# More row sums taken off ScalarE's own accumulator, a shorter way for the first head, and a root in seven steps instead of nine

## The chip, the cores and the metric

The kernel runs as one program on one core of one Trainium2 chip. The time is the device time of that core in microseconds (us), lower is better. Times of the kernel before are the median of three runs; beside them stands one further run under the hardware profiler, and all rows below come from that one.

## The reference, cut to what matters

One transformer layer on x of shape 8 x 1024 x 256 (batches, tokens, features), 16 heads of width 16, all in float32:

```python
x = x + attention(layernorm(x))
x = x + ffn(layernorm(x))

def layernorm(x):  return (x - mean) / sqrt(var + 1e-5)

def attention(x):                       # per head: q, k, v of 1024 x 16
    q_rot, k_rot = rotate(q), rotate(k) # rotary tables cos, sin
    num = exp(q_rot @ k_rot.T / 4)
    den = sum(exp(q @ k.T / 4), axis=-1)      # of the plain q and k, over all keys
    attn = where(causal, num / den, 0)
    return (attn @ v, heads side by side) @ Wout + bout

def ffn(x):     # shared expert (256 -> 128 -> 256, squared relu), plus routed experts
    ...         # weighted by trunc(softmax of the top two logits), which is 0 below 1.0
```

So each head needs two tables of exponentials: the denominator's, full 1024 x 1024 and only summed by row, and the numerator's, of which the causal half is used.

## The kernel before

**Tiling.** A batch is cut into 4 units of 4 heads (`G`, `HG`); 8 batches make 32 units. A unit is 50 steps (`NSTEP`), each one tile of 128 x 1024 scores: 32 "den" steps (4 heads x 8 blocks of 128 query rows, all 1024 keys) and 18 "num" steps that hold the causal half of the numerators in five chunks (`CHUNKS`; chunks 0 to 3 have one step for each head, chunk 4 has two heads in a step). Per step TensorE (PE) writes the tile into one of three score tiles in PSUM (`RING` = 3), and ScalarE (ACT) takes the exponential. A tile may be written again when the exponential three steps earlier is done.

**Row sums of the denominators.** A den step has two forms. In the first (L571) ACT writes the exponentials back in place and gives the row sum by its accumulator, which adds an instruction that reads the accumulator out. In the second (L569), for steps named in `SUMMED`, ACT writes the exponentials into one of two tiles in SBUF (`sum_tiles`, `SUM_SLOTS` = 2), and VectorE (DVE) adds the halves and sums them with its own accumulator (L1055, `sum_den`). That instruction stands in DVE's program three steps later (`SUM_LAG`). ACT waits before it writes a sum tile until the sum before last has been taken. `SUMMED` lists, for each of six kinds of unit (units 0 to 3 of a batch, the very last unit, the very first one), which of the 32 dens are summed so: 278 in the whole kernel, 746 go by the accumulator.

**Other work around the steps.** All engines walk the same 50 steps in their own fixed program; nothing is decided at run time. `ORDER`, `ORDER_FIRST`, `ORDER_LAST` say how dens and numerator chunks alternate. `PV_STEPS` says at which step PE multiplies a piece of a numerator chunk with v; `TAKE_Y` when DVE takes that sum out of PSUM. `SIDE` says at which step a side tile (one PSUM bank, `side`) is made by PE and taken by DVE: v, q and k of the next unit ("qk" and "turn" for the plain and rotated forms), the output projection ("acc"), the second layernorm's transposes ("t2"), the router and the shared expert of the batch before. `STATS2`, `STATS1`, `BIAS`, `GAP`, `BRANCH`, `RECIPROCALS` place single jobs of DVE, GpSimd (POOL) and ACT. `BUSY` and `WARM_UP` put dummy matmuls on PE.

**q and k.** For 6 products per score the float32 q and k are split into three bfloat16 parts (high, middle, low) by DVE, the last subtraction by POOL (L477). The parts go to DRAM (`scratch`, L376 on SyncE's DMA queue, SP) and come back as rows of `stack` in the order that the contraction over 96 rows wants: 6 DMAs for q and 6 for k for each of the plain and rotated forms (L393), 24 in a unit.

**The start.** Before batch 0: DVE takes the statistics of x and the inverse root (`inverse_root`, L959 on), writes the normalized blocks `xn` (L994), PE transposes them (L696) with dummy matmuls between (L627), ACT copies them (L592); PE makes q and k (L706), DVE splits them (L1338 to L1342), SP sends the two halves (L418). When both have landed, SP and ACT each issue 6 fills for heads 0 and 1 (`first_fill`, L346), then SP 6 for heads 2 and 3 of q. DVE meanwhile turns q and k and splits them into the same tile `parts` (L1330 to L1352), the second halves wait in SP's queue behind the fills (L418), then come 6 fills of k for heads 2 and 3 and the 12 fills of the rotated stack (L393). DVE enters batch 0 when both rotated halves have been sent (`rot_sent`).

**The inverse root.** `inverse_root` adds EPS, makes a first guess by integer arithmetic (three instructions in all) and does three Newton steps of three instructions each, with a drain behind each.

## Time and profile before

| what | us |
|---|---|
| median of 3 runs | 1618.52 (1616.33 to 1618.64) |
| the profiled execution: its own time | 1615.4 |
| its span, first to last instruction | 1613.7 |
| ACT busy | 1559.3 |
| PE busy (modelled ends) | 1508.5 |
| DVE busy | 1022.8 |
| POOL busy | 470.4 |

The granted TensorE clock has a mean of 0.997 over the span. How to read the profile: a row of a timeline gives start, duration, engine, source line, what is written and read, a count of merged instructions and, in brackets, the idle time of the engine before it with what ended it. A duration of ACT begins when the instruction is taken in, so two neighbours overlap; what a step costs is the distance between starts, its pitch. "<-PE scores L648" names the releaser of a wait; "issue" is time in which the engine waited for nothing that the profile shows.

### The profile page before, as it was taken

What the parts mean: (1) busy time and instruction counts of PE and PEld (TensorE: products, weight loads), DVE (VectorE), ACT (ScalarE), POOL (GpSimd) and SP (SyncE); (2) the same over time, 40 slices, a digit from 0 to 9 for tenths busy, and PEclk for the clock granted to TensorE, in tenths of its full rate; (3) what the DMA queues carried; (4) which work ended last, traced back from release to release, by engine and by line L of the source; (5) the groups of instructions that cost most, each with busy time, mean ns of one, the idle gap of its engine ahead of it and who ended that gap; (6) DMA issues with size and microseconds to landing.
All of it is one profiled execution on the core that took longest, in us unless ns stands there. A gap on an engine that the chain in (4) does not pass through costs nothing.

```text
span 1613.7 us, 26958 instructions
## 1 busy us (share of the span) xinstructions
PE 1508.5 (93%) x8670; PEld 624.2 (39%) x8670; DVE 1022.8 (63%) x2567; ACT 1559.3 (97%) x2373; POOL 470.4 (29%) x857
## 2 busy tenths in 40 slices
PE   7989999999999999999999999999999999999988
PEld 6334433333333333333333333433333333333325
DVE  5454656766567675677656676676666766566626
ACT  2999999999999999999999999999999999999995
POOL 3332233222332323323233223322233222332210
PEclk9999999999999999999999999999999999999999
DMA  5522233421434314343234333343243431433310
GB/s 165 159 92 86 85 118 115 134 93 59 134 119 134 102 47 134 118 125 118 69 106 131 115 105 99 115 127 95 89 145 105 131 99 62 129 120 116 106 39 27
DMA packets 95397, 172.14 MB, mean 107 GB/s; under 512 B 15696, under 2 KB 82256, under 8 KB 83152
## 3 DMA queue, kind: packets, MB, share of 16 engines
q1 hardware_dynamic: 94656, 169.55, 33.2%
q8 instruction: 72, 1.18, 0.3%
q10 hardware_dynamic: 592, 0.79, 0.2%
q14 instruction: 77, 0.63, 0.1%
HBM read 111.55 MB, written 58.72 MB: 106 GB/s over the span
## 4 chain that ended last, share of the span: by engine, by line
ACT 73%; issue 11%; PE 9%; DVE 3%; SPq 2%; DMA 1%; POOL 1%; DVEq 1%; POOLq 0%; ACTq 0%
ACT scores L571 37%; ACT probs L581 23%; ACT sum_tiles L569 11%; PE scores L648 3%; PE y_ps L677 2%; ACT probs L583 2%; SPq L393 2%; DMA qk_parts<-parts 1%; PE side L687 1%; PE side L627 1%; PE scores L655 1%; DVEq L958 0%; POOL probs L470 0%; PE side L706 0%; DMA stack<-qk_parts 0%
## 5 line engine op out<-in xcount | busy, mean ns | idle before, releaser
L571 ACT ACTIVATE scores<-scores 128x1024 f32<-128x1024 f32 x746 | 810.7, 1167 | 18.5 <-PE scores L648 18.3
L648 PE MATMUL scores<-stack 96*128 96x512 bf16 x2048 | 576.7, 382 | 37.6 <-ACT probs L581 12.4
L581 ACT ACTIVATE probs<-scores 128x1024 f32<-128x1024 f32 x512 | 497.9, 1158 | 0.2
L477 POOL TENSOR_TENSOR parts<-rest,parts 128x512 bf16<-128x512 f32 x124 | 161.2, 1300 | 748.0 <-DVE parts L1025 719.5
L655 PE MATMUL scores<-stack 96*128 96x512 bf16 (+3 forms) x1536 | 330.5, 327 | 36.9 <-ACT scores L571 16.2
L470 POOL TENSOR_SCALAR_AFFINE_SELECT probs<-probs 128x256 f32<-128x256 f32 (+1 forms) x640 | 245.2, 411 | 344.5 <-ACT probs L583 181.9
L677 PE MATMUL y_ps<-probs,v_sb 128*32 128x512 f32 (+3 forms) x3072 | 328.1, 499 | 1.0
L648 PEld LDWEIGHTS scores<-stack 96*128 96x128 bf16 x2048 | 151.2, 97 | 445.7 <-ACT scores L571 136.7
L569 ACT ACTIVATE sum_tiles<-scores 128x1024 f32<-128x1024 f32 x278 | 315.0, 1209 | 0.2 <-PE scores L648 0.2
L1055 DVE SCALAR_TENSOR_TENSOR sum_tiles<-sum_tiles 128x512 f32<-128x512 f32 x278 | 208.9, 763 | 88.9 <-ACT sum_tiles L569 80.0
L571 ACT ACTIVATION_READ_ACCUMULATOR scores<-scores 128x1 f32 x746 | 252.4, 338 | 0.0
L655 PEld LDWEIGHTS scores<-stack 96*128 96x128 bf16 x1536 | 123.5, 97 | 252.7 <-ACT scores L571 68.3
L706 PE MATMUL side<-xnt,w_qk 128*128 128x512 f32 x248 | 128.1, 597 | 0.0
L1034 DVE COPY rest<-side 128x512 f32<-128x512 f32 x62 | 42.9, 691 | 124.5 <-PE side L706 109.4
L677 PEld LDWEIGHTS y_ps<-probs,v_sb 128*32 128x32 f32 x3072 | 60.7, 108 | 150.5 <-issue 127.8
L583 ACT ACTIVATE probs<-scores 128x1024 f32<-128x1024 f32 x64 | 68.5, 1232 | 0.3 <-PE scores L655 0.3
L687 PE MATMUL side<-w_v,xnt 128*128 128x256 f32 x256 | 66.0, 379 | 2.4 <-DVE rot L1035 2.4
L722 PE MATMUL side<-w_o,y_sb 128*128 128x256 f32 x240 | 64.2, 390 | 0.0
L1043 DVE TENSOR_TENSOR turned<-turned,sin_sb 128x512 f32<-128x512 f32 x62 | 50.6, 816 | 19.4 <-POOL parts L477 19.4
L1025 DVE CAST parts<-rest 128x512 bf16<-128x512 f32 x124 | 53.0, 427 | 9.4 <-issue 0.4
L1005 DVE COPY v_sb<-side 128x128 f32<-128x128 f32 x128 | 28.2, 283 | 43.0 <-PE side L687 42.9
L511 POOL TENSOR_TENSOR tokens<-tokens,bias 128x256 f32<-128x256 f32 x64 | 53.2, 845 | 0.0
(145 smaller groups left out, 1238.9 us busy)
## 6 DMA issues: line engine op xcount, KB each, us to landing
stack<-qk_parts SPq DMA_DIRECT2D x756, 128.0 KB, 2.6
qk_parts<-parts SPq DMA_DIRECT2D x127, 384.0 KB, 2.6
out<-x_mid SPq DMA_DIRECT2D x32, 256.0 KB, 2.9
tokens<-in_L_attn_x SPq DMA_DIRECT2D x7, 1024.0 KB, 5.5
stack<-qk_parts SPq DMA_DIRECT2D x18, 64.0 KB, 2.3
tokens<-in_L_attn_x SPq DMA_DIRECT2D x2, 512.0 KB, 4.5
probs<-in_L_attn_Wqkv SPq DMA_DIRECT2D x1, 512.0 KB, 5.8
cos_sb<-in_cos SPq DMA_DIRECT2D x1, 512.0 KB, 6.5
```

What stands on the lines that cost most here:

```text
L470: nc.gpsimd.affine_select(out=v, in_=v, compare_op=ALU.is_ge, fill=0.0, base=0, pattern=pattern, channel_multiplier=-1).then_inc(masked, 1)
L477: nc.gpsimd.tensor_tensor(parts[:, t % 2, 2, :], rest[:, :], parts[:, t % 2, 1, :], ALU.subtract).then_inc(low_ready, 1)
L569: nc.scalar.activation(sum_tiles[:, k % SUM_SLOTS, :], src, ACT.Exp, scale=SCALE).then_inc(exp_done, 1)
L571: nc.scalar.activation(src, src, ACT.Exp, scale=SCALE, accum_out=den[:, g % 2, i, j:j + 1]).then_inc(exp_done, 1)
L581: nc.scalar.activation(probs[:, chunk % 2, j, :], src, ACT.Exp, scale=SCALE).then_inc(exp_done, 1)
L583: nc.scalar.activation(probs[:, chunk % 2, j:j + 2, 0:HALF], src.rearrange("p (a n) -> p a n", a=2), ACT.Exp, scale=SCALE).then_inc(exp_do ...
L648: mm = nc.tensor.matmul(tile[:, half * HALF:(half + 1) * HALF], q[:, j, i * P:(i + 1) * P], k[:, j, half * HALF:(half + 1) * HALF], start= ...
L655: mm = nc.tensor.matmul(tile[:, col:col + n], k[:, h, i * P:(i + 1) * P], q[:, h, q0:q0 + n], start=True, stop=True)
L677: mm = nc.tensor.matmul(y_ps[32 * j:32 * j + 32, o0:o0 + n], v_sb[:, i, h, :, :], probs[:, (5 * g + c) % 2, j, col:col + n], start=piece i ...
L687: mm = nc.tensor.matmul(side[:, i * D:(i + 1) * D], xnt[:, k, (2 * t + i) * P:(2 * t + i + 1) * P], w_v[:, k, :], start=k == 0, stop=k == ...
L706: mm = nc.tensor.matmul(side, w_qk[:, k, g, :], xnt[:, k, half * HALF:(half + 1) * HALF], start=k == 0, stop=k == KC - 1)
L1055: nc.vector.scalar_tensor_tensor(tile[:, 0:HALF], tile[:, 0:HALF], 0.0, tile[:, HALF:C], ALU.add, ALU.add, accum_out=den[:, g % 2, i, j:j ...
```

## The change

1. **Tables.** `SUMMED` names 344 dens instead of 278. With it `ORDER`, `ORDER_FIRST`, `ORDER_LAST`, `PV_STEPS`, `TAKE_Y`, `SIDE`, `RECIPROCALS`, `STATS1`, `STATS2`, `BIAS`, `GAP`, `BRANCH`, `BUSY` and `WARM_UP` get other numbers. By unit 0, 1, 2, 3, last, first the counts of summed dens go from 8, 6, 8, 14, 5, 7 to 7, 11, 9, 17, 8, 8.
2. **Start.** The six parts of head 0 of q and of k go from `parts` straight to the stack (`head_fill`), when the split is done, without DRAM. Heads 1 to 3 come from DRAM by 12 DMAs on SP (`heads_fill`). The rotated parts get a place of their own (`rot_parts`, in the second probability buffer), so the split of the rotated form waits for no DMA, and DVE enters batch 0 when the first head's rows are there.
3. **Root.** One Newton step with a scaled guess, then one step of third order: 3 + 4 instructions for 9.

```diff
+ROOT_SCALE = 0.375 ** 0.2
-ORDER = [5, (0,), 6, (1,), 2, (2,), 6, (3,), 6, (4,), 7]
-ORDER_FIRST = [15, (0,), 2, (1,), 3, (2,), 0, (3,), 1, (4,), 11]
+ORDER = [5, (0,), 4, (1,), 4, (2,), 6, (3,), 6, (4,), 7]
+ORDER_FIRST = [15, (0,), 0, (1,), 1, (2,), 1, (3,), 5, (4,), 10]
 SUMMED = [
-    (7, 11, 12, 16, 17, 20),
+    (2, 3, 5, 9, 11, 13, 19, 21, 24, 25, 26),
 SIDE = [
-    {0: ("xt", 1), 2: ("acc", 3), 4: ("xt", 2), 5: ("xt", 3), 9: ("qk", 0), 15: ("ffn", 4), 17: ("ffn", 5),
-     19: ("turn", 1), 22: ("qk", 2), 31: ("turn", 3), 34: ("ffn", 6), 39: ("ffn", 7)},
+    {0: ("xt", 1), 2: ("xt", 2), 4: ("acc", 3), 6: ("xt", 3), 8: ("qk", 0), 12: ("ffn", 4), 15: ("turn", 1),
+     19: ("ffn", 5), 22: ("qk", 2), 28: ("ffn", 6), 33: ("turn", 3), 35: ("ffn", 7)},
-WARM_UP = (22, 3, 3, 30, 22)
-BUSY = {(1, 4): 1, (1, 5): 1, (1, 6): 1, (1, 7): 1, (2, 7): 1, (2, 8): 1}
+WARM_UP = (19, 0, 3, 30, 13)
+BUSY = {(1, 3): 1, (1, 4): 1, (1, 5): 1, (1, 6): 1, (1, 7): 1, (1, 8): 1, (2, 6): 1, (2, 7): 1, (2, 8): 1}
-STATS2 = (1, 25)
+STATS2 = (1, 33)
...
+        rot_parts = probs[:, 1, 0:2, :].rearrange("p a n -> p (a n)").bitcast(BF16)[:, 0:2 * PARTS * HALF]
...
-        def first_fill(engine, a, term, heads, stacked):
+        def head_fill(engine, a, term):
             part = (Q_TERMS, K_TERMS)[a][term]
+            rows = parts[a * DH * HG:(a + 1) * DH * HG:HG, :, part, :]
+            engine.dma_start(stack[term:ROWS:TERMS, 0, 0, a, 0:C].rearrange("d (f t) -> d f t", f=2), rows).then_inc(first_stacked, 16)
+        def heads_fill(engine, a, term):
+            part = (Q_TERMS, K_TERMS)[a][term]
             src = scratch[0].rearrange("c s (d h) t -> c s d (h t)", h=HG)
-            cols = slice(heads * HG // 2 * C, (heads + 1) * HG // 2 * C)
-            engine.dma_start(stack[term:ROWS:TERMS, 0, 0, a, cols], src[part, a][:, cols]).then_inc(stacked, 16)
+            engine.dma_start(stack[term:ROWS:TERMS, 0, 0, a, C:HG * C], src[part, a][:, C:HG * C]).then_inc(plain_stacked[0], 16)
...
@@ SP @@
+            for term in range(TERMS):
+                head_fill(sp, 0, term)
             for half in range(2):
                 sp.wait_ge(first_sent[half], 16)
             sp.sem_inc(plain_sent, 32)
-            for term in range(TERMS):
-                first_fill(sp, 0, term, 0, first_stacked)
-            for term in range(TERMS):
-                first_fill(sp, 0, term, 1, plain_stacked[0])
+            for a in range(2):
+                for term in range(TERMS):
+                    heads_fill(sp, a, term)
             sp.wait_ge(low_ready, 4)
             first_parts(1, 1, rot_sent)
-            for term in range(TERMS):
-                first_fill(sp, 1, term, 1, plain_stacked[0])
             fill_stacks(0, 0, 1, rot_sent, rot_stacked)
@@ ACT @@
+                if j == 0 and first and chunk == 1:
+                    act.wait_ge(rot_sent, 32)
...
-            for half in range(2):
-                act.wait_ge(first_sent[half], 16)
+            act.wait_ge(low_ready, 2)
             for term in range(TERMS):
-                first_fill(act, 1, term, 0, first_stacked)
+                head_fill(act, 1, term)
@@ PE @@
-                            if step == ("den", HG // 2, 0):
+                            if step == ("den", 1, 0):
                                 pe.wait_ge(plain_stacked[0], FILLS * 16)
...
-            pe.wait_ge(first_sent[1], 16)
+            pe.wait_ge(low_ready, 2)
@@ DVE, inverse_root @@
-                for i in range(3):
-                    nc.vector.scalar_tensor_tensor(a, y, -0.5, y, ALU.mult, ALU.mult)
-                    settle()
-                    nc.vector.tensor_tensor(a, a, v, ALU.mult)
-                    settle()
-                    nc.vector.scalar_tensor_tensor(result if i == 2 else y, a, 1.5, y, ALU.add, ALU.mult)
-                    settle()
+                nc.vector.scalar_tensor_tensor(a, y, -0.5 * ROOT_SCALE, y, ALU.mult, ALU.mult)
+                nc.vector.tensor_tensor(a, a, v, ALU.mult)
+                nc.vector.scalar_tensor_tensor(y, a, 1.5 * ROOT_SCALE, y, ALU.add, ALU.mult)
+                nc.vector.tensor_tensor(a, y, y, ALU.mult)
+                nc.vector.tensor_tensor(a, a, v, ALU.mult)
+                nc.vector.scalar_tensor_tensor(v, a, -10 / 3 * ROOT_SCALE ** 2, a, ALU.add, ALU.mult)
+                nc.vector.scalar_tensor_tensor(result, v, 5 * ROOT_SCALE ** 4, y, ALU.add, ALU.mult)
...
@@ DVE, before batch 0 @@
-                dve.wait_ge(first_sent[half], 16)
-                first_split(half, rot_of[half])
-            dve.wait_ge(rot_sent, 32)
+                first_split(half, rot_of[half])
+            for half in range(2):
+                dve.wait_ge(first_sent[half], 16)
+            dve.wait_ge(first_stacked, FILLS * 16)
```

(In the new root each instruction still has its drain behind it.)

**Where instructions stand, three places.** SP's queue from the first sent halves on, before; the shapes are the destination's rows and columns, `qk_parts` is `scratch`:

```order
L418 DMA qk_parts<-parts 128x3x512 x2
L346 DMA stack<-qk_parts 16x2048 x12
L418 DMA qk_parts<-parts 128x3x512
L346 DMA stack<-qk_parts 16x2048 x6
L393 DMA stack<-qk_parts 16x4096 x12
L376 DMA qk_parts<-parts 128x3x512 x3
```

And now:

```order
L426 DMA qk_parts<-parts 128x3x512 x2
L348 DMA stack<-parts 16x2x512 x6
L354 DMA stack<-qk_parts 16x3072 x12
L426 DMA qk_parts<-probs 128x3x512
L401 DMA stack<-qk_parts 16x4096 x12
L384 DMA qk_parts<-parts 128x3x512 x3
```

The queue has as many DMAs as before; six read `parts` directly, and the second rotated half now stands behind 18 fills and not behind 12, with none between it and the rotated stack.

PE from its first dummy matmul to the first scores, before:

```order
L627 MATMUL side<-ident 128x128 x22
L696 MATMUL scores<-ident,xn 128x128 x4
L627 MATMUL side<-ident 128x128 x3
L706 MATMUL scores<-xnt,w_qk 128x512 x4
L627 MATMUL side<-ident 128x128 x52
L648 MATMUL scores<-stack 128x512 x4
L706 MATMUL side<-xnt,w_qk 128x512
```

(the rows of 4 transposes and 3 dummies come four times) and now:

```order
L635 MATMUL side<-ident 128x128 x19
L704 MATMUL scores<-ident,xn 128x128 x16
L635 MATMUL side<-ident 128x128 x3
L714 MATMUL scores<-xnt,w_qk 128x512 x4
L635 MATMUL side<-ident 128x128 x43
L656 MATMUL scores<-stack 128x512 x2
L714 MATMUL side<-xnt,w_qk 128x512
```

There are 21 dummy matmuls fewer, none between the transposes, and the first side tile stands one step earlier.

ACT in the second half of unit 1 (here of batch 0), from the third numerator chunk (before: from the fourth den behind it) on, before:

```order
L569 ACTIVATE sum_tiles<-scores 128x1024 x2
L571 ACTIVATE scores,den<-scores 128x1024
L581 ACTIVATE probs<-scores 128x1024 x4
L571 ACTIVATE scores,den<-scores 128x1024
L569 ACTIVATE sum_tiles<-scores 128x1024
L571 ACTIVATE scores,den<-scores 128x1024 x4
L583 ACTIVATE probs<-scores 128x2x512 x2
L571 ACTIVATE scores,den<-scores 128x1024 x12
```

And now:

```order
L590 ACTIVATE probs<-scores 128x1024 x4
L576 ACTIVATE sum_tiles<-scores 128x1024
L578 ACTIVATE scores,den<-scores 128x1024 x5
L590 ACTIVATE probs<-scores 128x1024 x4
L576 ACTIVATE sum_tiles<-scores 128x1024
L578 ACTIVATE scores,den<-scores 128x1024
L576 ACTIVATE sum_tiles<-scores 128x1024
L578 ACTIVATE scores,den<-scores 128x1024 x2
L576 ACTIVATE sum_tiles<-scores 128x1024
L592 ACTIVATE probs<-scores 128x2x512 x2
L576 ACTIVATE sum_tiles<-scores 128x1024 x2
L578 ACTIVATE scores,den<-scores 128x1024 x10
```

Dens that went through L571 (now L578) go through L569 (now L576), six in this stretch where three stood; never more than two follow one another.

## Rows read from the trace of the kernel before

**Rows 1.** ACT's groups: line, operation, tiles, count | busy us, mean ns | idle before.

```profile
L571 ACT ACTIVATE scores<-scores 128x1024 f32<-128x1024 f32 x746 | 810.7, 1167 | 18.5 <-PE scores L648 18.3
...
L569 ACT ACTIVATE sum_tiles<-scores 128x1024 f32<-128x1024 f32 x278 | 315.0, 1209 | 0.2 <-PE scores L648 0.2
```

**Rows 2.** Timeline of ACT in unit 3 of batch 5.

```profile
1158.74 1.25 ACT L571 ACTIVATE scores<-scores 128x1024 f32<-128x1024 f32 x1
...
1159.77 3.99 ACT L581 ACTIVATE probs<-scores 128x1024 f32<-128x1024 f32 x4
1163.38 1.29 ACT L569 ACTIVATE sum_tiles<-scores 128x1024 f32<-128x1024 f32 x1
1164.28 1.30 ACT L571 ACTIVATE scores<-scores 128x1024 f32<-128x1024 f32 x1
```

**Rows 3.** Timeline of ACT: the first and the last of the 1600 steps.

```profile
34.56 1.01 ACT L571 ACTIVATE scores<-scores 128x1024 f32<-128x1024 f32 x1 [10.84 <-PE scores L648]
...
1590.46 1.03 ACT L571 ACTIVATE scores<-scores 128x1024 f32<-128x1024 f32 x1
```

**Rows 4.** Timeline of all engines at the start.

```profile
5.26 8.07 PE L627 MATMUL side<-ident 128*128 128x128 f32 x44 [5.26 <-POOL ident L454]
...
11.54 1.38 DVE L994 TENSOR_SCALAR xn<-tokens,mean_var,rstd 128x256 f32<-128x256 f32 x4
...
13.17 0.60 PE L696 MATMUL scores<-ident,xn 128*128 128x128 f32 x4
...
17.87 3.67 PE L706 MATMUL scores<-xnt,w_qk 128*128 128x512 f32 x8
...
24.11 0.69 DVE L1342 TENSOR_TENSOR parts<-y_sb,parts 128x512 bf16<-128x512 f32 x1 [0.51 <-issue]
...
27.45 7.75 SPq L346 DMA_DIRECT2D stack<-qk_parts  x12
27.46 4.04 ACTq L346 DMA_DIRECT2D stack<-qk_parts  x6
...
34.66 1.16 POOL L539 TENSOR_TENSOR parts<-y_sb,parts 128x512 bf16<-128x512 f32 x1 [3.16 <-DVE parts L1334]
...
38.59 0.69 DVE L1034 COPY rest<-side 128x512 f32<-128x512 f32 x1 [4.02 <-DMA qk_parts<-parts]
...
40.04 8.26 SPq L393 DMA_DIRECT2D stack<-qk_parts  x12
...
41.54 1.01 ACT L571 ACTIVATE scores<-scores 128x1024 f32<-128x1024 f32 x1 [2.90 <-PE scores L648]
```

**Rows 5.** Timeline of ACT: the first numerator steps of the kernel.

```profile
52.74 3.76 ACT L581 ACTIVATE probs<-scores 128x1024 f32<-128x1024 f32 x4
```

**Rows 6.** Busy time (count) of PE, PEld, DVE, ACT, POOL by stretch; PEclk, DMA share, GB/s.

```profile
1057.99:1106.44 48.45, 45.61 (x274) 17.90 (x273) 34.24 (x98) 48.45 (x78) 13.31 (x25) 1.00 0.41 126
...
93.30:96.70 3.40, 3.40 (x6) 1.32 (x6) 3.10 (x5) 2.79 (x4) 1.20 (x2) 0.50 0.36 120
```

**Rows 7.** The page: DVE's group that takes the sums.

```profile
L1055 DVE SCALAR_TENSOR_TENSOR sum_tiles<-sum_tiles 128x512 f32<-128x512 f32 x278 | 208.9, 763 | 88.9 <-ACT sum_tiles L569 80.0
```

**Rows 8.** Timeline of DVE in unit 1 of batch 5: the second layernorm's last root instruction.

```profile
1086.14 0.17 DVE L974 SCALAR_TENSOR_TENSOR rstd<-root 128x8 f32<-128x8 f32 x1
1086.39 1.38 DVE L994 TENSOR_SCALAR xn<-x_mid,mean_var,rstd 128x256 f32<-128x256 f32 x4
```

**Rows 9.** Timeline of SP around the change from batch 5 to batch 6.

```profile
1193.38 0.50 SPq L376 DMA_DIRECT2D qk_parts<-parts  x1
1196.64 8.28 SPq L393 DMA_DIRECT2D stack<-qk_parts  x12
```

**Rows 10.** Timeline of POOL there: the low part of the rotated second half.

```profile
1186.76 1.16 POOL L477 TENSOR_TENSOR parts<-rest,parts 128x512 bf16<-128x512 f32 x1 [4.09 <-ACT probs L581]
```

**Rows 11.** Timeline of ACT there: third step of batch 6, and its first numerators.

```profile
1205.24 1.01 ACT L571 ACTIVATE scores<-scores 128x1024 f32<-128x1024 f32 x1 [0.18 <-PE scores L648]
...
1208.18 2.85 ACT L581 ACTIVATE probs<-scores 128x1024 f32<-128x1024 f32 x3
```

More of the change, by code:

```diff
@@ L418, in first_parts @@
                 sp.dma_start(scratch[kind, :, :, :, half * HALF:(half + 1) * HALF].rearrange("c s r t -> (s r) c t"),
-                             parts[:, half, :, :]).then_inc(sent, 16)
+                             (parts, rot_parts)[kind][:, half, :, :]).then_inc(sent, 16)
             sp.sem_inc(out_sent, 1)
@@ L538, in _ @@
                 pool.wait_ge(middle_ready, half + 3)
[L539 removed]
+                nc.gpsimd.tensor_tensor(rot_parts[:, half, 2, :], rest_of[half], rot_parts[:, half, 1, :], ALU.subtract
                                         ).then_inc(low_ready, 1)
```

62 lines of the change are left out of this document (32 added, 30 removed), and 17 rows, old and new, of tables (PV_STEPS, SUMMED).

## The prediction

> **What bounds the kernel now.** First I read the busy shares in the table: ACT is busy 1559.3 of 1613.7 us, more than any other engine. ACT's groups [rows 1] then show that it hardly waits: its main group idled 18.5 us in all, of which 10.84 stand before the very first score tile [rows 3]. So I took the timeline of ACT and looked at the distance between starts, since durations overlap. In an undisturbed stretch [rows 2] a den through the accumulator (L571) takes 1159.77 - 1158.74 = 1.03 us until the next step starts, four numerator steps 3.61, so 0.90 each, and a den through a sum tile (L569) 1164.28 - 1163.38 = 0.90. 746 steps of the first kind and 1600 - 746 = 854 of the others [rows 1] make 746 x 1.03 + 854 x 0.90 = 1537 us. From the first step to the start of the last are 1555.9 us [rows 3], some 1538 less the last step's own, so about 19 us in the 1600 steps are losses. Known among them are 2.90 at 41.54 [rows 4] and, in the stretch of 3.4 us in which the granted clock was 0.50, the lower of TensorE's two levels, 3.40 - 2.79 = 0.6 or more of idle ACT [rows 6]. The kernel's time is therefore three parts: 34.6 us until the first exponential, 1556 of steps paced by ACT, and 23 behind them, a chain through DVE, PE and ACT.
>
> **Sums moved.** 344 - 278 = 66 dens change from L571 to L569. Each saves ACT 1.03 - 0.90 = 0.13 us (0.126 with one more digit of the same starts: 1.029 and 0.903), so 66 x 0.126 = **8.3 us**, all on the path, since ACT sets it. The cost lies on DVE: 208.9 / 278 = 0.75 us for each [rows 7], 50 us over the kernel. The fullest unit is unit 1: DVE was busy 34.24 of 48.45 us [rows 6] and gets 5 sums more, so 38.0 us or 78%. That is cover enough on average; ACT pays only if a sum tile is wanted again before DVE has come to it. ACT's order shows never more than two such dens in a row, with numerators or accumulator dens behind them, as before.
>
> As a counterweight, the Trainium skill ("ScalarE: Activation LUTs", What ACT_TABLE_LOAD costs) gives an activation with immediate scale and bias 186 ns + 0.833 ns a column and 93 ns of overlap between neighbours. For 1024 columns that is 946 ns a step; with the trace's 1.03 for the accumulator form the saving would be an estimate of 0.083 a den, 5.5 us for 66. The trace does not agree: its pitch is 0.90, for numerators and sum tiles alike, and I go by the trace.
>
> **The start.** Five steps, each from [rows 4] unless said. (a) The root loses two instructions. One takes 1086.39 - 1086.14 = 0.25 us from start to start [rows 8], so `xn` starts 0.5 us earlier, at 11.05, and its first pair is done at 11.05 + 0.69 = 11.7. (b) PE's first dummies ended at 13.33 and held the transposes back. With 19 for 22 they end 3 x 2 records earlier, at the warm rate some 0.14 us each, so about 12.5: 0.8 us. Without the dummies between them the four blocks of transposes, 4.70 us up to the q and k product at 17.87, become a chain of 0.6 us of PE and 0.7 us of DVE for the third and fourth block, with some 0.3 us of hand-over each; I work it out as 3.6 us. Both together bring the product forward by 1.9 us; the bounds are 0.8 (only the dummies at the front count) and 2.5 (the path through DVE alone). (c) The parts of q and k are ready at 24.80 before, so at 22.9. Until now the fills then waited for two landings and started at 27.45. Now SP sends the second half and then issues 6 head fills, ACT its 6, from 23.3 and 23.0 on. A fill's issue takes 7.75 / 12 = 0.65 us, so the last ends near 27.2. Before, the last issue on ACT ended at 31.50 and the first exponential came 3.06 later; now that gives **30.3** instead of 34.56. The new fills move 1 KB pieces instead of 4 KB, from SBUF and not from DRAM; no row shows such a fill, so between 1 us less and 2 us more for the landing. (d) Behind them 12 fills of the other heads are issued until 27.2 + 7.8 = 35.0 and land by 37.4; step 8, which needs them, comes at 30.3 + 8 x 1.03 = 38.5, and PE wants them a little earlier: no loss, or up to 1 us. The wait of 2.90 at 41.54 goes: DVE entered batch 0 at 38.59, held by the rotated parts, while PE waited for it to take the first side tile. Its chain and POOL's last low part (35.82) come 1.9 earlier, so DVE starts at 34.0; PE meets the next side tile at step 5, near 35, so some tenths remain. (e) What is late next is the rotated stack. The second rotated half is now behind 18 fills: issued at 35.0 (its low part is ready at 33.9), landed and waited for 2.7 us as before, then 12 fills in 8.3 us from 37.7 to 46.0, landed near **48.1**; before they were issued from 40.04 to 48.30. ACT would be ready for the first numerator at 30.3 + 13 x 1.03 + 2 x 0.90 + 0.4 = 45.9 and waits for it until about 48.8. Before, it came at 52.74 [rows 5]. The start as a whole thus gives **4.0 us**, not the 4.3 plus 2.9 that (c) and (d) would; its bounds are 2.0 (if (b) gives 0.8, and landings are slower) and 5.0.
>
> **Losses in the steps.** Three things can add or take. ACT's 0.18 us before the third step of a batch [rows 11] with the longer pitches around it recur at each batch, and they are PE's: side tiles stand there in both kernels. One more dummy matmul stands in unit 2 beside steps where PE is just ahead, and three places in unit 1 likewise; one is about 0.14 x 2 = 0.28 us. In the first unit numerator chunks now follow each other sooner, and chunk 2 at step 24 needs v's product of chunk 0, of which the last piece stands on PE at that same step. I take 0.5 us for the first unit and 0.1 to 0.15 for each of seven batches, together **+1.3 us**. The lower bound is -5 (most of the small waits vanish), the upper +7 (1 us a batch).
> The step for the rotated half of the next batch's first unit moves from 31 to 33, 1.9 us later. That costs nothing: POOL's low part was done at 1187.92 [rows 10], but SP sent it at 1193.38, behind the plain fills, [rows 9], so 5.4 us of room. Its fills ended at 1204.92 and the numerator ran at 1208.18 [rows 11]; landing takes 2 to 3 us, so there is about a microsecond in hand, and this does not change, as the plain half (step 22) stays where it was.
>
> **The end.** Behind the last exponential one root stands on the chain: **-0.5 us**. In the other batches the root is on DVE beside ACT and worth nothing. The last unit's new order ends on 11 dens instead of 7, with the same five end tiles in the loop; I see no gain or loss above 0.5 in it.
>
> **The sum.** -8.3 - 4.0 + 1.3 - 0.5 = **-11.5 us**. On the profiled execution: span 1613.7 to 1602.2, its own time 1615.4 to 1603.9. That execution is 3.1 us below the median of the three runs, 1618.52, for which I forecast **1607.0**.
>
> **Rivals.**
> (1) *The start gives back more.* If fills out of SBUF in 1 KB pieces are slow, or the rotated stack comes only as before (48.30 issued), the start is worth 0.5 to 1: 1610. For it speaks that the queue of SP is as long as before; against it that its waits for landings before the fills are gone.
> (2) *PE takes part of the saving.* PE is busy 45.61 of 48.45 us in unit 1 [rows 6], and with ACT 0.63 us faster there only 2.2 us are left. If half of the 8.3 is waited for at PE, 1611. Against it: ACT did not idle in that stretch at all (48.45 of 48.45), and PE's ends are modelled.
> (3) *Slower: DVE too late for the sum tiles.* In unit 1 the layernorm block (5 us of DVE) moves from step 25 to 33, in front of the sums of steps 35 and 37, and a third follows at 40. If PE's transposes hold DVE up between them, the sum of step 35 is not taken when ACT wants its tile. The price is the delay itself, once in each of seven batches. It cancels the whole gain from 12.8 / 7 = 1.8 us on; at 3 us it gives 1618.5 - 12.8 + 21 = 1627. Against it: DVE's program has nothing that waits between step 28 and this block, so DVE can run it early and be through before step 35.
> (4) *The clock.* Fewer dummies run at the start, and PE idles for up to 1 us or more before the first scores. The trace shows the clock at 0.50 for 3.4 us at 93.3, amid work, at a price of 0.6 us or more on ACT [rows 6]. One such stretch more at 1 us gives 1608; at the start, where PE is on the path, the q and k product of 3.67 us [rows 4] at half the clock takes that much more, and gives 1611. The Trainium skill ("TensorE: Matmul & The Clock Gate", Part 1: The HAM clock gate) says that the clock halves when the array has been idle and comes back with work; the row at 93.3, with PE busy 3.40 of 3.40 us, does not look like idleness, so I give it little.
>
> **How the numbers follow.** Forecast 0.62 (own range 1603 to 1610), rival 1 0.12, rival 2 0.13, rival 3 0.05, rival 4 0.08. The range 1601.5 to 1612.5 takes in the forecast's bounds, rivals 1, 2 and 4, and the scatter of 2.3 us between the three runs; outside are rival 3 and the extremes. About 0.2% (3.2 us) is what a measurement can tell from no change, so faster means below 1615.3: 0.91. Within 0.2% 0.05, where several bounds meet; slower 0.04, which is rival 3.
>
> **What the profile after would show.** ACT's in-place group at 680 and the sum group at 344; pitches of 1.03 and 0.90 unchanged; the first exponential near 30.3; the first numerator near 48.8 with a wait of some 3 us on the stack in front of it; idle of ACT in the later batches no more than before; `xn` 0.5 us earlier; DVE busy some 50 us more, less 34 root instructions of 0.17. It is wrong if ACT waits for DVE's sums in unit 1, if the first numerator comes after 51, or if pitches of the new sums are longer than 0.90.

## The result, and the profile after

| | before | after |
|---|---|---|
| median | 1617.42 us (4 runs, 1614.39 to 1618.64) | 1601.70 us (4 runs, 1600.98 to 1603.35) |
| the profiled execution: its own time | 1615.4 | 1600.98 |
| its span | 1613.7 | 1599.4 |
| first exponential / first numerator | 34.56 / 52.74 | 29.21 / 47.45 |
| last step's start to the end of the span | 23.29 | 22.70 |
| ACT / DVE / POOL / PE busy | 1559.3 / 1022.8 / 470.4 / 1508.5 | 1551.9 / 1064.9 / 506.7 / 1508.3 |

The ratio is 0.9908, with an interval of 0.9896 to 0.9919. The medians are 15.7 us apart (the ratio makes it 14.9), where 11.5 were forecast. The time lies just inside the range, 0.2 us above its lower end. The two profiled executions are 14.4 us apart; the other 1.3 us are what the medians lie above them, 2.0 before and 0.7 after.

The groups of the page after, ACT's two kinds of dens and DVE's sums (line, engine, operation, tiles, count | busy, mean ns | idle before), to be held against [rows 1, 7]:

```profile
L578 ACT ACTIVATE scores<-scores 128x1024 f32<-128x1024 f32 x680 | 752.9, 1225 | 10.4 <-PE scores L656 10.2
...
L576 ACT ACTIVATE sum_tiles<-scores 128x1024 f32<-128x1024 f32 x344 | 405.0, 1243 | 0.0
...
L1070 DVE SCALAR_TENSOR_TENSOR sum_tiles<-sum_tiles 128x512 f32<-128x512 f32 x344 | 257.3, 756 | 87.6 <-ACT sum_tiles L576 81.2
```

66 dens changed sides, DVE took 48.4 us more of sums, and ACT never once idled before a sum tile. Of the 10.4 us of idle before L578, 7.9 stand before the first step. A den through the accumulator still takes 1.029 us from its start to the next, every other step 0.903.

The start, timeline of all engines (to be held against [rows 4, 5]):

```profile
11.06 2.92 DVE L1009 TENSOR_SCALAR xn<-tokens,mean_var,rstd 128x256 f32<-128x256 f32 x8
...
15.47 3.67 PE L714 MATMUL scores<-xnt,w_qk 128*128 128x512 f32 x8
...
22.02 4.07 ACTq L348 DMA_DIRECT2D stack<-parts  x6
...
26.52 7.71 SPq L354 DMA_DIRECT2D stack<-qk_parts  x12
...
28.58 0.60 PE L656 MATMUL scores<-stack 96*128 96x512 bf16 x2
...
37.23 7.44 SPq L401 DMA_DIRECT2D stack<-qk_parts  x12
...
46.81 0.61 PE L663 MATMUL scores<-stack 96*128 96x512 bf16 x2 [3.59 <-DMA stack<-qk_parts]
...
47.45 1.02 ACT L590 ACTIVATE probs<-scores 128x1024 f32<-128x1024 f32 x1 [1.93 <-PE scores L663]
...
49.96 1.02 ACT L590 ACTIVATE probs<-scores 128x1024 f32<-128x1024 f32 x1 [1.49 <-PE scores L663]
```

Everything comes earlier, by 2.4 us at the product for q and k and by 5.3 at the first exponential and at the first numerator. The last two rows show something that the prediction had not expected at this place: after the wait for the stack, one numerator step is 2.5 us from the next instead of 0.90. The stretch behind it (busy time and count of PE, PEld, DVE, ACT, POOL; granted clock, DMA share, GB/s) shows why:

```profile
47.35:50.76 3.41, 3.41 (x7) 1.25 (x6) 0.00 (x0) 1.82 (x2) 0.00 (x0) 0.50 0.36 120
```

PE had idled 3.59 us for the rotated stack, and then runs at the lower level of its clock, busy all the time, with ACT busy only 1.82 of 3.41 us.

I took all 1600 steps apart: the start of each to the start of the next, less the undisturbed pitch of its kind in the kernel before (1.029 and 0.903, for all runs alike). What is left is called losses below.

| us | before | after | difference |
|---|---|---|---|
| first exponential at | 34.56 | 29.21 | -5.35 |
| 66 pitches of 0.126 less | | | -8.3 |
| losses, batch 0, unit 0 | 3.81 | 6.50 | +2.69 |
| losses, batch 0, unit 1 | 2.15 | 0.94 | -1.21 |
| losses, all other units | 12.17 | 10.56 | -1.61 |
| behind the last step's start | 23.29 | 22.70 | -0.59 |

They add up to the 14.4 within rounding. All losses together are 18.1 before and 18.0 after. Of the 6.5 us in unit 0 after, 3.4 stand behind the first numerator; before, it was 0.6 of 3.8.

### The profile page after: what moved, and what is told of

The parts are those of the page before. It is cut to its first block, busy times and chain, and to the rows that moved or that the text cites. A ratio compares the mean times of both kernels' runs of the same rounds, so it can differ in the third digit from the quotient of the medians.

```text
span 1599.4 us, 27029 instructions
## 1 busy us (share of the span) xinstructions
PE 1508.3 (94%) x8670; PEld 626.1 (39%) x8670; DVE 1064.9 (67%) x2665; ACT 1551.9 (97%) x2307; POOL 506.7 (32%) x857
## 4 chain that ended last, share of the span: by engine, by line
ACT 72%; issue 14%; PE 11%; DVE 1%; SPq 1%; DVEq 0%; DMA 0%; POOL 0%; ACTq 0%; POOLq 0%
ACT scores L578 33%; ACT probs L590 22%; ACT sum_tiles L576 15%; PE scores L656 3%; ACT probs L592 2%; PE scores L663 2%; PE side L695 2%; PE y_ps L685 2%; PE side L635 1%; SPq L354 0%; SPq L401 0%; PE side L714 0%; DVEq L966 0%; SPq L348 0%; PE scores L843 0%
## 5 line engine op out<-in xcount | busy, mean ns | idle before, releaser
L578 ACT ACTIVATE scores<-scores 128x1024 f32<-128x1024 f32 x680 | 752.9, 1225 | 10.4 <-PE scores L656 10.2
L590 ACT ACTIVATE probs<-scores 128x1024 f32<-128x1024 f32 x512 | 504.4, 1212 | 4.8 <-PE scores L663 4.2
L576 ACT ACTIVATE sum_tiles<-scores 128x1024 f32<-128x1024 f32 x344 | 405.0, 1243 | 0.0
L484 POOL TENSOR_TENSOR parts<-rest,parts 128x512 bf16<-128x512 f32 x124 | 175.5, 1415 | 689.2 <-DVE parts L1040 689.2
L477 POOL TENSOR_SCALAR_AFFINE_SELECT probs<-probs 128x256 f32<-128x256 f32 (+1 forms) x640 | 270.4, 450 | 352.5 <-ACT probs L592 179.0
L1070 DVE SCALAR_TENSOR_TENSOR sum_tiles<-sum_tiles 128x512 f32<-128x512 f32 x344 | 257.3, 756 | 87.6 <-ACT sum_tiles L576 81.2
L578 ACT ACTIVATION_READ_ACCUMULATOR scores<-scores 128x1 f32 x680 | 269.7, 397 | 0.0
L592 ACT ACTIVATE probs<-scores 128x1024 f32<-128x1024 f32 x64 | 69.1, 1242 | 0.1
L1058 DVE TENSOR_TENSOR turned<-turned,sin_sb 128x512 f32<-128x512 f32 x62 | 44.0, 710 | 19.9 <-POOL parts L484 18.8
L714 PEld LDWEIGHTS side<-xnt,w_qk 128*128 128x128 f32 x248 | 46.6, 191 | 14.3 <-DVE v_sb L1020 0.3
```

The costliest lines, as they stand in the source:

```text
L477: nc.gpsimd.affine_select(out=v, in_=v, compare_op=ALU.is_ge, fill=0.0, base=0, pattern=pattern, channel_multiplier=-1).then_inc(masked, 1)
L484: nc.gpsimd.tensor_tensor(parts[:, t % 2, 2, :], rest[:, :], parts[:, t % 2, 1, :], ALU.subtract).then_inc(low_ready, 1)
L576: nc.scalar.activation(sum_tiles[:, k % SUM_SLOTS, :], src, ACT.Exp, scale=SCALE).then_inc(exp_done, 1)
L578: nc.scalar.activation(src, src, ACT.Exp, scale=SCALE, accum_out=den[:, g % 2, i, j:j + 1]).then_inc(exp_done, 1)
L590: nc.scalar.activation(probs[:, chunk % 2, j, :], src, ACT.Exp, scale=SCALE).then_inc(exp_done, 1)
L592: nc.scalar.activation(probs[:, chunk % 2, j:j + 2, 0:HALF], src.rearrange("p (a n) -> p a n", a=2), ACT.Exp, scale=SCALE).then_inc(exp_do ...
```

## The experiments

They ran in three groups of four, e1 to e4, e5 to e8 and e9 to e12, each group on one chip with its own runs of the kernel before; the ratios are against those. Spans, waits and losses are those of the one profiled execution of each.

**e1: the new places with the old list of sums.** The changed kernel with the lines of `SUMMED` put back (278 sums):

```diff
-    (2, 3, 5, 9, 11, 13, 19, 21, 24, 25, 26),
+    (7, 11, 12, 16, 17, 20),
```

and the other five lines likewise.

> The changed kernel with the old list of summed dens (278 again), everything else new. If each summed den is worth the difference of ACT's pitches (1.029 - 0.903 = 0.126 us), the 66 dens go back to the accumulator and the span grows by 8.3 us, from 1599.4 to about 1607.7; the first exponential stays at 29.2 and losses of ACT stay near 18. If the rest of the tables (order, side tiles) carry the gain and the sums little, the span stays within 3 us of 1599.4.

Measured: 1641.36 us, ratio 1.0137 (1.0117 to 1.0158): 40 us slower than the changed kernel, not 8. Losses are 49.8 us; in batches 1 to 7 unit 1 loses 4.6 to 4.8 us each where the changed kernel loses 0.02. The timeline in unit 1 of batch 6:

```profile
1297.47 0.69 DVE L1070 SCALAR_TENSOR_TENSOR sum_tiles<-sum_tiles 128x512 f32<-128x512 f32 x1 [1.52 <-ACT sum_tiles L576]
...
1298.99 4.04 ACT L590 ACTIVATE probs<-scores 128x1024 f32<-128x1024 f32 x4
...
1299.17 0.64 DVE L1001 BATCH_NORM_AGGREGATE mean_var<-stats 128x2 f32<-128x6 f32 x8
...
1304.00 1.09 PE L738 MATMUL side<-ident,xn 128*128 128x128 f32 x4 [3.05 <-DVE xn L1009]
...
1305.98 1.01 ACT L578 ACTIVATE scores<-scores 128x1024 f32<-128x1024 f32 x1 [2.95 <-PE scores L656]
```

And the same place in the changed kernel:

```profile
1266.93 0.64 DVE L1001 BATCH_NORM_AGGREGATE mean_var<-stats 128x2 f32<-128x6 f32 x8
...
1269.97 4.05 ACT L590 ACTIVATE probs<-scores 128x1024 f32<-128x1024 f32 x4
...
1270.42 1.38 DVE L1009 TENSOR_SCALAR xn<-x_mid,mean_var,rstd 128x256 f32<-128x256 f32 x4
...
1271.79 0.60 PE L738 MATMUL side<-ident,xn 128*128 128x128 f32 x4
```

Against the same four numerators of ACT, DVE begins the layernorm block 3.04 us before them in the changed kernel, and 0.18 us behind them in e1. The first row of e1 shows what holds it, a sum that waits 1.52 us for ACT: the old list sums the dens 16 and 17, here steps 28 and 29, and these two sums stand in DVE's program directly ahead of the block. Not the number of sums decides, but whether one that must wait for ACT stands ahead of work that PE waits for.

**e2: the new list of sums with the old places.** The kernel before with nothing but the new `SUMMED` (344 sums).

> The kernel before with the new list of 344 summed dens and nothing else. Pitch theory: span 1613.7 - 8.3 = 1605.4, losses of ACT still 18. Rival: the new sums need the new order and the moved side tiles, and without them DVE comes too late for its two sum tiles; then ACT shows waits with DVE as the releaser, 1 us or more a batch, and the span is 1610 to 1625.

Measured: 1653.71 us, ratio 1.02 (1.0169 to 1.0231), losses 67.1. The sums alone save 8.3 us of ACT's pitches and make this kernel some 37 us slower (1653.71 against 1617.08; one of its four executions took only 1645.88). ACT's group, and the place in unit 3 where it idles (batch 5):

```profile
L569 ACT ACTIVATE sum_tiles<-scores 128x1024 f32<-128x1024 f32 x344 | 367.0, 1109 | 12.2 <-DVE sum_tiles L1055 11.8 <-PE scores L648 0.3
```

```profile
1193.39 0.69 DVE L1034 COPY rest<-side 128x512 f32<-128x512 f32 x1 [2.65 <-PE side L706]
...
1197.05 0.68 DVE L1055 SCALAR_TENSOR_TENSOR sum_tiles<-sum_tiles 128x512 f32<-128x512 f32 x1
...
1197.83 1.02 ACT L569 ACTIVATE sum_tiles<-scores 128x1024 f32<-128x1024 f32 x1 [1.68 <-DVE sum_tiles L1055]
```

Here the wait of rival 3 can be seen: a side tile that comes late from PE (2.65) holds DVE, the sum is queued behind its split, and ACT waits 1.68 us for its sum tile, in seven of eight batches. In unit 1 more is lost, 3.8 to 5.3 us in six of the batches; there PE waits some 2.2 us for DVE's `x_mid`. The list of sums is all that was changed, so the sums bring this about; which of them holds `x_mid` back was not traced. In batch 6:

```profile
1304.85 1.13 PE L722 MATMUL side<-w_o,y_sb 128*128 128x256 f32 x4 [2.21 <-DVE x_mid L1116]
```

This run also shows something about the start, which is here the same code as in the kernel before:

```profile
33.02 1.01 ACT L571 ACTIVATE scores<-scores 128x1024 f32<-128x1024 f32 x1 [10.12 <-PE scores L648]
```

The first exponential comes 1.54 us earlier than the 34.56 of before. The granted clock rose at 8.9 and not at 11.4, the product for q and k started at 17.05 and not at 17.87, and the last fill on ACT's queue landed 1.6 us behind the end of its issue and not 2.4. So the profiled execution of before had a late start, and a part of what the start seems to gain against it is scatter.

**e3: the start alone.** The kernel before with part 2 of the change (`head_fill`, `heads_fill`, `rot_parts`, the new waits) and the new `WARM_UP`; root and tables old.

> The kernel before with the new start alone (head 0 straight from SBUF, rotated parts apart, fewer dummy matmuls), old tables and old root. The first exponential should come at about 29.7 (29.2 plus the 0.5 us of the root, as the dummies no longer hold the transposes back). If the first numerators then are bound by the rotated stack, SP's queue decides: it lands near 47.2 and the first numerator comes near 48, against 52.74 before: 4.5 to 5 us gained. If the gain of the start came through the new order of the first unit, this one gains at most 2.

Measured: 1613.24 us, ratio 0.9968 (0.9955 to 0.9981): 5.2 us faster by the ratio, 3.8 by the medians, 3.2 by the spans. The first exponential comes at 30.05, the first numerator at 49.95, against 29.21 and 47.45 with everything. The difference between the two kernels grows from 0.8 to 2.5 us mainly through one place:

```profile
35.46 1.53 PE L695 MATMUL side<-w_v,xnt 128*128 128x256 f32 x4 [2.79 <-DVE rot L1043]
...
37.88 1.01 ACT L578 ACTIVATE scores<-scores 128x1024 f32<-128x1024 f32 x1 [3.75 <-PE scores L656]
...
40.04 1.01 ACT L578 ACTIVATE scores<-scores 128x1024 f32<-128x1024 f32 x1 [1.04 <-PE scores L656]
```

The old table has v's side tile at step 3 and PE waits there for DVE, still at the rotated split; the new one has it at step 5. Behind the idle of PE the granted clock is 0.50 from 36.05 to 39.46.

**e4: the root alone**, in the kernel before.

> The kernel before with the shorter root alone. Adding up instructions (2 fewer of 0.24 us, once at the start and once at the end) gives 1.0 us. The other reading is that the 22 dummy matmuls, which ended at 13.3 while the first blocks were ready at 12.3, swallow the first half: then the first exponential stays at 34.56 and only the tail shortens, from 23.3 to 22.8, 0.5 us in all.

Measured: 1615.41 us, ratio 0.9985 (0.9976 to 0.9995); the profiled pair differs by 1.5 us. At the end the half microsecond is there: 22.80 behind the last step's start instead of 23.29. At the start `xn` comes 0.46 earlier:

```profile
11.08 1.43 DVE L1002 TENSOR_SCALAR xn<-tokens,mean_var,rstd 128x256 f32<-128x256 f32 x4
12.68 0.60 PE L697 MATMUL scores<-ident,xn 128*128 128x128 f32 x4
```

but PE's 22 dummies still stand ahead of the transposes and hold them until 12.68, instead of 13.17. That they end earlier at all is not the root's doing: the granted clock rose at 10.3 in this execution and at 11.4 in that of before. The first exponential came at 33.39, 1.17 earlier than in before, where I had expected no change; e2, with the old root, came to it at 33.02, so this is the scatter of the start and not the root. With the old dummies the root stays hidden at the start.

**e5: 66 sums fewer, places kept.** The changed kernel with 66 dens taken out of the new lists and none put elsewhere, for instance

```diff
-    (2, 3, 5, 9, 11, 13, 19, 21, 24, 25, 26),
+    (2, 5, 11, 19, 24, 26),
```

> The changed kernel with 66 of its 344 summed dens simply dropped from its own lists (5 of 11 in unit 1, 3 of 17 in unit 3, 3 in the last and 2 in the first unit), so 278 again, and no sum at a place where none stood. Theory: a sum is worth 0.126 us on ACT and nothing else; the span grows by 8.3 us to 1607.7 and ACT's losses stay within 1 us of 18.0. Rival: taking sums away moves DVE's work as well and brings losses back, as the old list did; then losses grow by several us and the span passes 1612.

Measured: 1611.82 us, ratio 0.9961 (0.9947 to 0.9976). Its span is 1608.8, 9.4 more than the changed kernel's: 8.3 of pitches, 0.8 of losses, 0.3 at the end. The pitches are the same, 1.0295 and 0.9034, so a sum on DVE is worth 0.126 us where its place is free. The prediction had two prices for the 66 sums, 8.3 us by the trace's pitches and an estimate of 5.5 by the Trainium skill ("ScalarE: Activation LUTs", What ACT_TABLE_LOAD costs); the run agrees with the trace.

**e6: two sums moved.** The changed kernel, 344 sums, two of unit 1 in other places (steps 28 and 29 of the unit instead of two behind the block):

```diff
-    (2, 3, 5, 9, 11, 13, 19, 21, 24, 25, 26),
+    (2, 3, 5, 9, 11, 13, 16, 17, 24, 25, 26),
```

> The changed kernel, with two of unit 1's eleven summed dens in another place: dens 16 and 17 (steps 28 and 29) instead of 19 and 21 (steps 35 and 37). The count is the same, 344. Theory: DVE takes the sum of step 29 at its place 32, right in front of the second layernorm (place 33), and must wait there for ACT to reach step 30, so the layernorm comes some 3 us later, PE waits for its first block at step 34 and ACT runs dry: unit 1 loses 4 to 5 us in each of 7 batches, part of it through a halved clock, and the span is 1599.4 + 30 = 1630 or so. Rival: the loss with the old list came from the sums as a whole (their number in units 0 and 3, or the pace of ACT), then two moved sums cost under 5 us in all.

Measured: 1632.84 us, ratio 1.0079 (1.005 to 1.0107): 31 us more than the changed kernel for two numbers of a list (16 sums, two in each batch), with 3.6 to 5.4 us lost in unit 1 of each of the batches 1 to 7 and the granted clock at 0.50 for 3.4 or 6.8 us there. In batch 5:

```profile
1096.32 0.69 DVE L1070 SCALAR_TENSOR_TENSOR sum_tiles<-sum_tiles 128x512 f32<-128x512 f32 x1 [1.41 <-ACT sum_tiles L576]
...
1098.02 0.64 DVE L1001 BATCH_NORM_AGGREGATE mean_var<-stats 128x2 f32<-128x6 f32 x8
...
1102.51 1.08 PE L738 MATMUL side<-ident,xn 128*128 128x128 f32 x4 [2.71 <-DVE xn L1009]
...
1104.49 1.01 ACT L578 ACTIVATE scores<-scores 128x1024 f32<-128x1024 f32 x1 [2.61 <-PE scores L656]
```

The same rows as in e1, with every other table as in the changed kernel. The two sums alone bring e1's loss in unit 1 back, and that is its cause.

**e7: PE kept busy in its gap.** The changed kernel with 16 dummy matmuls ahead of PE's wait for the rotated stack:

```diff
+                            if first and g == 0:
+                                keep_busy(16, y_ps)
```

> The changed kernel with 16 dummy matmuls on PE (into the bank of the head products, not yet in use) in front of its wait for the first rotated stack, where PE idled 3.6 us and the granted clock then fell to 0.50 for 3.4 us. Theory: the idle time brings the fall; with PE busy the clock stays at 1.00, the two waits of 1.5 and 0.75 us behind the first numerator go, and the losses of the first unit fall from 6.5 to about 4 us, the span by 2.5 to 1597. Rival: the fall has nothing to do with the idle time (before the change it came at 93.3, amid work) and stays, or comes a little later, at the same price: span 1599 to 1600.

Measured: 1603.17 us, ratio 0.99 (0.988 to 0.9919). The granted clock is 1.00 from 8.7 us on and through all 1600 steps, and the waits behind the first numerator are 0.27 and 0.27 instead of 1.49 and 0.75:

```profile
48.16 1.02 ACT L590 ACTIVATE probs<-scores 128x1024 f32<-128x1024 f32 x1 [2.64 <-PE scores L663]
49.45 1.02 ACT L590 ACTIVATE probs<-scores 128x1024 f32<-128x1024 f32 x1 [0.27 <-PE scores L663]
```

```profile
47.35:50.76 3.41, 3.25 (x11) 1.45 (x12) 0.35 (x1) 2.07 (x3) 0.00 (x0) 1.00 0.52 180
```

So at this place the fall follows PE's idle time. Unit 0 of batch 0 lost 5.6 us instead of 6.5, forecast 4. The time itself did not come down: in this execution the 12 fills were issued in 8.29 us and not in 7.44, which brought the first numerator 0.7 later, and ACT's longer pitches (last section) come to some 2.3 us.

**e8: two fills on ACT's queue.** The changed kernel, in which ACT issues the last two of the 12 fills of heads 1 to 3:

```diff
-                for term in range(TERMS):
+                for term in range(TERMS - 2 * a):
...
+            for half in range(2):
+                act.wait_ge(first_sent[half], 16)
+            for term in range(TERMS - 2, TERMS):
+                heads_fill(act, 1, term)
```

> The changed kernel with the last two of the twelve fills for heads 1 to 3 issued by ACT, which has nothing to issue between 26.1 and 28.7, instead of SP. Theory: the first numerator is bound by SP's queue of single issues of 0.63 us; two fewer let the second rotated half go out when its low part is ready (33.0 instead of 34.3), the rotated stack lands near 45.5 and the first numerator is exponentiated at 46.2 instead of 47.45: 1.2 us less. Rival: the bound is the transfers themselves; then landings only bunch and the first numerator stays at 47.4.

Measured: 1602.94 us, ratio 0.9897 (0.9877 to 0.9917). SP sends the rotated half at 33.44 instead of 34.27, and the first numerator comes at 46.47, a wait of 0.54 instead of 1.93:

```profile
46.47 1.02 ACT L590 ACTIVATE probs<-scores 128x1024 f32<-128x1024 f32 x1 [0.54 <-PE scores L667]
```

PE idled 2.21 us before it and the clock did not fall there. It fell at 86.1, for 6.8 us, behind idle times of PE of at most 0.42:

```profile
84.40:91.20 6.80, 5.96 (x13) 1.61 (x14) 5.25 (x11) 6.55 (x9) 1.56 (x2) 0.63 0.17 58
91.20:98.00 6.80, 6.80 (x33) 2.98 (x32) 4.43 (x10) 5.33 (x9) 1.88 (x2) 0.87 0.17 59
```

Unit 0 lost 3.5 instead of 6.5 us, unit 1 then 2.9 instead of 0.9, so two thirds of the 3 us were given back.

**e9: the three put together.** e8's edit, nine dummies at e7's place, and the dummies of `BUSY` in unit 1 of batch 0 too:

```diff
-                if not first and (unit_of(b, g), s) in BUSY:
+                if (not first or g == 1) and (unit_of(b, g), s) in BUSY:
```

> The changed kernel, in which ACT issues the last two of the twelve fills for heads 1 to 3 (so the rotated half and the rotated stack behind it leave SP's queue some 0.9 us earlier), PE gets nine dummy matmuls ahead of its wait for the rotated stack, and the dummies that units 1 and 2 have in every other batch also stand in unit 1 of batch 0. Theory, the clock falls because PE idled: first numerator near 46.5 instead of 47.45, granted clock 1.00 behind it and through unit 1 of batch 0; the losses of unit 0 of batch 0 come down from 6.5 to about 3 us and those of unit 1 stay near 0.9, so 3 us less than the unchanged control of this call. Rival, a fall somewhere in batch 0 comes anyway and only moves: less than 1 us.

Measured: 1599.90 us (1599.45 to 1601.59), ratio 0.9883 (0.9868 to 0.9898), 2.7 below the control e12 of the same group, whose five runs all lie above all five of these; 3 were expected. The clock is 1.00 through all 1600 steps, in the two stretches in which it fell in the kernels above as well:

```profile
47.35:50.76 3.41, 3.23 (x13) 1.19 (x11) 1.29 (x3) 2.87 (x4) 0.00 (x0) 1.00 0.34 115
```

```profile
84.40:91.20 6.80, 6.61 (x28) 3.03 (x28) 5.28 (x11) 6.80 (x9) 1.53 (x1) 1.00 0.17 58
91.20:98.00 6.80, 6.57 (x40) 2.27 (x37) 5.02 (x12) 6.80 (x12) 1.93 (x2) 1.00 0.19 61
```

Which of the three edits keeps the clock up in the second stretch is not shown: e7, without the dummies of unit 1, had 1.00 there too, and so had the changed kernel.

The first numerator came at 47.13, not at 46.5. The fills began at 36.20, 1.0 earlier than in the changed kernel, but the last of them landed 2.8 us behind its issue instead of 2.1. Losses of unit 0 are 4.5, of unit 1 0.9.

**e10: 14 sums more.** The changed kernel with dens 9 and 13 of unit 0 summed too, in batches 1 to 7:

```diff
-    (6, 7, 11, 15, 24, 25, 28),
+    (6, 7, 9, 11, 13, 15, 24, 25, 28),
```

> The changed kernel with two more dens of unit 0 summed by DVE (dens 9 and 13 in order, steps 17 and 25 of the unit) in batches 1 to 7: 14 sums more, 358 in all. Theory, a sum is worth 0.126 us wherever no instruction of DVE that waits for PE or ACT is caught behind it and ahead of a step that PE needs: 14 x 0.126 = 1.8 us less than the control, losses of unit 0 unchanged at about 0.6 us a batch. Rival, unit 0 has no room left either, and DVE's side tile at step 19 or 28 comes late: losses in unit 0 grow by 0.3 us a batch or more, which takes the gain back.

Measured: 1602.75 us, ratio 0.99 (0.9885 to 0.9915), the same as the control's 1602.61. In the profiled pair, which ran at the same pitches, its span is 1.1 us less: 1.8 of pitches, 0.4 by an earlier start, less 0.8 more of losses (0.71 instead of 0.59 in a typical unit 0: step 26 takes 0.1 to 0.2 longer) and 0.3 at the end. So the trace has part of the 1.8, and the losses grow by 0.12 a batch, less than half of what the rival asked for; in the medians of five runs nothing of it shows. Whether 14 more sums are worth a microsecond stays open.

**e11: e9 and e10 together.**

> Both edits together: the shorter start with its dummies, and 14 sums more. Theory: the two act in different places and add up, about 4.5 us less than the control, near 1597. Rival: 2 us or less, if either edit gives nothing.

Measured: 1600.63 us (1598.41 to 1602.38), ratio 0.9884 (0.9868 to 0.99). The profiled execution, 1596.6 us of span, is the shortest of all; its first numerator stands at 45.99, the losses of unit 0 of batch 0 at 3.5:

```profile
45.99 1.02 ACT L590 ACTIVATE probs<-scores 128x1024 f32<-128x1024 f32 x1 [0.47 <-PE scores L667]
```

The median is 2.0 below the control, where 4.5 were expected, and not below e9's. The start's gain is there in both, that of the 14 sums in neither median.

**e12: the changed kernel once more**, the control of that group.

> The changed kernel unchanged, as the control of this call. Expected: 1600 to 1603, ratio to the kernel before near 0.990, first exponential 29.2, first numerator 47.5, granted clock 0.50 behind it. If ACT's distance between starts differs here from the 1.0295 us of the first execution, that is the scatter between executions, 1.5 to 2.5 us over 1600 steps.

Measured: 1602.61 us (1602.39 to 1603.13), ratio 0.9898 (0.9883 to 0.9912). The first exponential comes at 29.59, the first numerator at 47.70, and behind it the clock is at 0.50 again, now from 48.5 on:

```profile
48.60:51.90 3.30, 3.30 (x7) 1.27 (x6) 0.83 (x2) 1.23 (x3) 0.00 (x0) 0.50 0.21 68
```

## Why the prediction was right, and where it was off

The time is in the stated range, but by 0.2 us, and it lies below the forecast's own 1603 to 1610; no rival covers it, since all four make the kernel slower than forecast. The mechanisms below were right in the main. But the start, the losses and the step from the profile to the median all came out better than their terms, and the four executions spread over 2.4 us, two of them below 1601.5. That the median fell on the inner side of the bound is luck.

**What bounds the kernel**: right. ACT's pitches carried the sum, and with them the main term.

**Sums moved, -8.3**: right. The pitches are unchanged, 66 of them changed kind, and e5 gives the same 8.3 the other way round. DVE's price was 48.4 us, forecast 50.

**The start, -4.0**: its mechanism right, its size short by 1.3 and 0.3 beyond its own bound of 5.0; the first numerator came at 47.45 and not at 48.8. Against e4, whose start is the old one with the new root, the gain at the first numerator is 4.4 (51.84 to 47.45), so up to 0.9 of the 5.3 is the late start of the one execution of before. (a) `xn` at 11.06, as worked out. (b) was worth 2.4, not 1.9. The chain from the first transpose to the product takes 15.47 - 11.90 = 3.57, as worked out, but the dummies were over at 11.9 and not at 12.5, because the granted clock rose at 9.8 in this execution and at 11.4 in that of before. In e12 it rose at 11.0, and the first exponential came 0.37 later than in after. (c) The landing of a fill out of SBUF, the unknown of that step, took some 2.0 us from its issue, and 2.3 in the old form from DRAM: not slower, which closes rival 1. The rows of the first head were there at 27.6, and the first scores came at 28.58: PE's own dummies, which run until then, took the last microsecond. Fewer of them there was not tried. (d) The wait of 2.90 is gone, and four waits of 0.15 to 0.18 are left. e3 shows that this part belongs to the new tables and not to the new start: with the old ones a wait of 3.75 stands there. I had put it down to the earlier split alone. (e) was right in what is late next, the rotated stack: landed at 46.76, forecast 48.1, since (b) and (c) came earlier and the fills took 7.44 instead of 8.3. The wait in front of it was 1.93 us, forecast 3.

**Losses, +1.3**: this is the term that was mis-sized, it came out at -0.1. For the later batches the forecast of 0.1 to 0.15 each fits: a typical batch has 1.33 before and 1.43 after. For batch 0 it was wrong in both directions. Unit 0 lost 2.7 more instead of 0.5; 1.7 of it is the stretch of half clock behind PE's idle time (e7), which the prediction had looked for before the first scores and not before the first numerator. Elsewhere 3.3 came back: 1.2 in unit 1 of batch 0, where the stretch at 93.3 that I had read [rows 6] was not there after, 1.4 in unit 2 of batch 2, where before had a like one at 533.6, and 0.8 in the last unit. I had left their price in the sum without asking whether they would stay, and had read it too low: ACT waited 0.61 us in the stretch at 93.3 and 0.53 more right behind it, 1.1 in all and not 0.6.

**The end, -0.5**: 0.59 measured; e4 alone gives 0.49.

**From the profile to the median.** I put the whole 3.1 us between the profiled execution and the median of before on top of the forecast. After it was 0.7. Of the 5.3 us by which the forecast was too high, 2.9 are the sum's and 2.4 this step's. In the last group the kernel before ran between 1614.74 us (mean granted clock 0.998) and 1623.42 (0.993), the changed kernel between 1602.39 and 1603.13 (0.998 to 0.999): the longer executions of before had the lower mean clocks, so its scatter goes with stretches of half clock, and the changed kernel has fewer of them. No run here shows which of its edits does that.

**The rivals.** (1) fell, with the landings above. (2) fell: ACT waited no more for PE in the later batches. (3) did not come, but the mechanism is real and dear: e6 shows it with two numbers of a list, e2 with ACT waiting for DVE itself. The argument against it, that nothing in DVE's program waits between step 28 and the layernorm block, was the one that counts. The price is higher than the one I gave, the delay once in each batch: in e6 a delay of 3.3 us against the numerators costs 3.6 to 5.4, with a fall of the clock beside it each time. (4) came, in another place. Behind 3.59 us of idle PE the clock stood at 0.50 for 3.4 us; with the idle time filled (e7, e9, e11) or cut to 2.21 us (e8) it did not. The Trainium skill ("TensorE: Matmul & The Clock Gate", Part 1: The HAM clock gate) says that idleness of the array lowers the clock, and here the trace agrees. I had set that rule aside because PE was busy in all of the stretch at 93.3. But PE is busy 45.61 of 48.45 us at the full clock [rows 6], so at half of it there is always work; to find a cause, one has to look at what PE did ahead of the fall. The length of one idle time does not decide alone, though. In e2, PE's 2.21 us of idle ahead of 1304.85 are followed by a fall at 1305.97, and 2.40 us in the kernel before, ahead of 39.94, by none. In the 9 us ahead of 93.3 PE was idle for 2.5 us in all, but never for more than 0.51 at a time. What brings a fall there in some executions and not in others, no run shows.

## What to carry to other kernels

Taking work off the engine that sets the pace is worth its full price per instruction only if the helper's instruction never waits ahead of something that a third engine needs: look at what stands behind each such instruction in the helper's queue, since two sums of each batch in the wrong place (16 in the kernel) cost here nearly four times what 66 in the right place save. When a start is shortened, look for the wait that is now the longest on PE and for the clock behind it, and fill it or shorten it. And put only that part of the losses into the sum that comes again in each batch: a loss that one execution has once is scatter.

## What the runs showed of the hardware that I had not expected

- ACT's pitch differs between executions, for all steps of one alike. A numerator step takes 0.9034 us in before, after, e5, e9 and e11 and 0.9042 to 0.9043 in the nine others; a den by the accumulator takes 1.0295 or, in e6, e7, e8, e10 and e12, 1.0307 to 1.0318. Over 1600 steps that is 0.8 to 2.4 us. e9 to e12 ran one after the other on one chip and have both kinds. So 1.7 of the 2.5 us between the profiled spans of e9 and e12 are pitch and no merit of e9, and its own gain is nearer 1 us: 0.9 there, and 1.1 against the first execution of after, at the same pitch. How much of the 2.7 between the medians is pitch, and why the pitch differs, no run shows.
- A stretch of half clock costs ACT between some 1.1 us (at 93.3, before: waits of 0.61 and 0.53) and 1.7 us (at 47.35, after: waits of 1.49 and 0.75 against two of 0.27 in e7), and it comes again in every batch if the wait that causes it does: e1's mean granted clock is 0.983.
- The same 12 fills on SP's queue (the rotated stack of batch 0) took 7.44 or 7.45 us to issue in all ten other executions with the new start and 8.29 in e7.
- The same start differs by 1.5 us between executions: the first exponential came at 34.56, 33.39 and 33.02 with the old start (before, e4, e2), with the clock up from 11.4, 10.3 and 8.9 on. With the new start it came between 29.15 and 29.60 in all executions with the new root, though the clock rose anywhere from 8.7 to 11.0.
